# Moving four quantizations into the projection loop of a state-space and FP4 feed-forward layer

## The reference, cut to what matters

```python
def fp4_quant_dequant(x):
    xb = x.reshape(shape[:-1] + (shape[-1] // BLOCK, BLOCK))     # BLOCK = 16
    scale = jnp.max(jnp.abs(xb), axis=-1, keepdims=True) / 6.0
    xn = xb / scale
    idx = jnp.searchsorted(_MID, jnp.abs(xn))
    q = _GRID[idx] * jnp.sign(xn) * scale
...
xn = _layernorm(x, axis=-1)
x = x + _L0_attn_ref(xn, ...) + _L0_ffn_ref(xn, ...)
# _L0_attn_ref: u = layernorm(u, ...); zxbcdt = einsum('bld,od->blo', u, l2norm(in_proj_w)) * DIM ** (-0.5)
# _L0_ffn_ref:  gate = fp4_linear(x, w_gate); y = fp4_linear(x, w_up); fp4_linear(silu(gate) * y, w_down)
```

## Time and profile before

| | us |
|---|---|
| three runs | 13649.85, 13658.45, 13591.88 (median 13649.85) |
| profiled execution, time | 13639.79 |
| its slowest core (core 5), span | 13638.0 |
| the eight cores' spans | 13525.6 to 13638.0 |
| stage 1 on core 5 | about 262 to 2935 |
| busy in the whole span | DVE 6887.7 (51%), PE 6484.3 (48%), PEld 2707.2, ACT 2420.9, POOL 1499.5 |

### The profile page before, as it was taken

The page is one execution under the profiler, slowest core; times in us unless marked ns, Lnnn a source line. Parts: engine busy times, 40 slices in busy tenths (PEclk is TensorE's granted clock), DMA queues, the critical chain, the costliest instruction groups (busy, mean ns, idle before and its releaser), DMA issues.

```text
span 13638.0 us, 120366 instructions; the slowest of 8 cores (13525.6 to 13638.0 us)
## 1 busy us (share of the span) xinstructions
PE 6484.3 (48%) x27434; PEld 2707.2 (20%) x27434; DVE 6887.7 (51%) x21998; ACT 2420.9 (18%) x3604; POOL 1499.5 (11%) x1616
## 2 busy tenths in 40 slices
PE   2555555544555455545554014444444444440678
PEld 1222222212222222222221001111112111110233
DVE  4433333334443444344435986666666666668200
ACT  2222222222222222222222111111111111111000
POOL 1111111100000000000001111111111111111000
PEclk8777777775556555655565556666666666665777
DMA  2111111110001000100010010000000000001232
GB/s 65 45 45 46 46 46 46 45 62 27 30 27 48 27 30 27 48 27 27 30 48 23 31 34 12 12 14 22 12 12 24 12 12 24 12 9 51 98 125 102
DMA packets 285044, 505.71 MB, mean 37 GB/s; under 512 B 35506, under 2 KB 207410, under 8 KB 282306
## 3 DMA queue, kind: packets, MB, share of 16 engines
q1 hardware_dynamic: 235842, 333.82, 7.7%
q0 software_dynamic: 48512, 164.18, 3.1%
HBM read 294.17 MB, written 199.81 MB: 36 GB/s over the span
## 4 chain that ended last, share of the span: by engine, by line
PE 28%; DVE 25%; issue 21%; DMA 14%; ACT 8%; SPq 2%; DVEq 1%; ACTq 0%; POOL 0%; POOLq 0%
DMA s_siluz<-stg_ev 4%; PE p_u L1533 4%; PE p_d L1656 4%; DMA s_xbc<-stg_ev 4%; PE p_g L1524 2%; PE p_sc L1423 2%; PE ptrA L397 2%; DMA hqt<-s_hqT 2%; PE p_seg L1423 2%; DVE hb L1553 2%; DVE q_amax L281 1%; PE ptr L397 1%; ACT q_sg L260 1%; ACT q_absx L259 1%; DVE xbcw L1390 1%
## 5 line engine op out<-in xcount | busy, mean ns | idle before, releaser
L1533 PE MATMUL p_u<-wut,xq 128*128 128x512 bf16 (+1 forms) x3072 | 867.9, 440 | 1422.0 <-DVE hb L1553 1422.0
L716 PE MATMUL pmm<-xhT,wnt 128*128 128x512 bf16 (+1 forms) x4352 | 1149.5, 412 | 736.0 <-ACT stg_ev L733 718.7
L368 POOL TENSOR_TENSOR q_ss<-q_sg,q_sclh 128x512 f16<-128x512 f16 (+3 forms) x560 | 785.5, 1420 | 4899.8 <-DVE q_rcp L291 4714.5
L1524 PE MATMUL p_g<-wgt,xq 128*128 128x512 bf16 (+1 forms) x3072 | 843.9, 428 | 18.4 <-ACT gs L1545 12.1
L1656 PE MATMUL p_d<-wdt,hqt 128*128 128x512 bf16 x2816 | 734.6, 433 | 202.1 <-DVE ostg L1670 201.2
L1545 ACT ACTIVATE gs<-p_g 128x512 bf16<-128x512 f32 (+1 forms) x384 | 213.6, 556 | 3035.9 <-DVE hb L1553 1668.5
L1533 PEld LDWEIGHTS p_u<-wut,xq 128*128 128x128 bf16 x3072 | 343.5, 115 | 1882.3 <-issue 1696.4
L1240 DVE SCALAR_TENSOR_TENSOR attb<-eb,ldtT,scoresM 128x256 bf16<-128x256 bf16 x1024 | 455.0, 485 | 500.3 <-ACT eb L1226 415.2
L1553 DVE TENSOR_TENSOR hb<-p_u,gs 128x512 f32<-128x512 f32 (+1 forms) x384 | 246.6, 642 | 884.7 <-PE p_u L1533 884.7
L1341 POOL TENSOR_TENSOR g2scr<-xbcw 128x256 bf16<-128x256 bf16 x512 | 313.4, 612 | 3418.3 <-DVE xbcw L1327 3418.3
L716 PEld LDWEIGHTS pmm<-xhT,wnt 128*128 128x128 bf16 (+1 forms) x4352 | 408.6, 103 | 1342.2 <-issue 1010.2
(11 more groups left out here) (232 smaller groups left out, 13100.6 us busy)
## 6 DMA issues: line engine op xcount, KB each, us to landing
s_hqT<-hqTb POOLq DMA_DIRECT2D x16, 2816.0 KB, 11.5
hqt<-s_hqT SPq DMA_DIRECT2D x16, 2816.0 KB
xbcw<-s_xbc SPq DMA_DIRECT2D x272, 128.8 KB
s_xbc<-stg_ev SPq DMA_DIRECT2D x272, 128.0 KB
ubuf<-u SPq DMA_DIRECT2D x16, 2048.0 KB
s_siluz<-stg_ev POOLq DMA_DIRECT2D x256, 128.0 KB, 2.0
zld<-s_siluz SPq DMA_DIRECT2D x16, 2048.0 KB
ubp<-u SPq DMA_DIRECT2D x64, 512.0 KB
```

Source lines behind the costliest of these rows:

```text
L368: ii = nc.gpsimd.tensor_mul(q["ss"][:, CS[i]], q["sg"][:, CS[i]], q["sclh16"][:, GS[i]].unsqueeze(2) .broadcast_to([128, hb, 16]))
L716: nc.tensor.matmul(pm[0:rows, :], wnt[:, k * F + ft * 128: k * F + ft * 128 + rows], xhT[:, k * TILE:(k + 1) * TILE], start=(k == 0), stop ...
L1524: i = nc.tensor.matmul(p_g[:, 0:nn], xqb[:, k * TILE + mt * 128: k * TILE + (mt + 1) * 128], wgt[:, k * FFI + i0: k * FFI + i1], start=(k ...
L1533: i = nc.tensor.matmul(p_u[:, 0:nn], xqb[:, k * TILE + mt * 128: k * TILE + (mt + 1) * 128], wut[:, k * FFI + i0: k * FFI + i1], start=(k ...
```

## The change

The four calls of `emit_quant_full` leave their place ahead of the loop over `ft`. They are wrapped in a function `emit_q1` and called at the top of the iterations ft = 1, 9, 17 and 25, ahead of the matmuls of that iteration. In each engine's queue their instructions now stand behind those of ft 0, 8, 16 and 24. `prev_qsg_ac`, for which the next tile's normalization waits, is taken after the last one as before.

```diff
--- before.py
+++ after.py
@@ -687,23 +687,26 @@
                                     pe_waits=[XH_M])
             prev_xht_pe = cnt["pe"]
             qtrans = []
-            for sl4 in range(4):
+
+            def emit_q1(sl4):
                 QS_VE = emit_quant_full(xn[:, sl4 * 1024:(sl4 + 1) * 1024],
                                         qd[:, sl4 * 1024:(sl4 + 1) * 1024],
                                         1024, q1, first_wait=XN_M)
-                if sl4 == 3:
-                    prev_qsg_ac = cnt["ac"]
-                mt = sl4
                 blocks = [(qd[:, sl4 * 1024 + j * 128:
                               sl4 * 1024 + (j + 1) * 128],
-                           xnqT[:, j * TILE + mt * 128:
-                                j * TILE + (mt + 1) * 128])
+                           xnqT[:, j * TILE + sl4 * 128:
+                                j * TILE + (sl4 + 1) * 128])
                           for j in range(8)]
                 qtrans.append((blocks, QS_VE))
+                return cnt["ac"]
 
             xbv = xbc_s.rearrange("(s c p) l -> s c p l", s=SEQ, c=NCT)
             szv = siluz_s.rearrange("(t z p) n -> t z p n", t=NT, z=NZT)
             for ft in range(NFT):
+                if ft % 8 == 1 and ft < 32:
+                    qac = emit_q1(ft // 8)
+                    if ft // 8 == 3:
+                        prev_qsg_ac = qac
                 rows = 128 if ft < 33 else 16
                 pm = (pmm0, pmm1, pmm2)[ft % 3]
                 @block.tensor
```

## The result

The changed kernel takes 13142.4 us, median of 10 runs (13101.7 to 13202.7), against 13623.1 for ten of the kernel before (13566.3 to 13671.3): a ratio of 0.9648, 95% interval 0.9625 to 0.967, 481 us or 3.5% less. The forecast was 13150 us, in the range 13070 to 13290.

A forecast was written before the change was run, and what follows sets the result against it. Waits, not a busy engine, set normalization and input projection, with stores one at a time pacing the ft loop. 34.2-3.0-0.4 = 30.8 us per tile, times 16, took 493 from 13639.8: 13147, stated as 13150, range 13070 to 13290.

The forecast's parts named there:

- The 34.2 us ahead of the second store: Start of each tile's store loop: POOL stores ft 1 at 1472.7 instead of 1506.89, 34.2 us earlier.
- The 3.0 us at ft 9: POOL's queue: quantization 1's `ss` products stand ahead of ft 9's store, 3.0 us lost per tile.
- Stores beside DVE's quantization: POOL's stores: some 8 per tile run beside DVE's quantization, 0.05 us each, 0.4 us lost per tile.
- The bound that I kept for stores beside `aa`: First half of two quantizations: stores waiting out both `aa` would cost 4 us per tile, kept for the range.
- Quantizations 2 and 3 at nothing: Loop's second half, stores on SP: Abs and Sign just fit between ACT's evictions and were costed at nothing.
- The cover of 6 us: End of the loop: quantization 3 ends after 15.1 us while the loop goes on for 21, leaving 6 us.
- Sum: Stage 1: 34.2-3.0-0.4 = 30.8 us saved per tile, times 16: 493 us, giving 13147 us.
- the first: Rival, store loop: more slow transfers, 102 us, 13250, or PE at a reduced clock, 13200; chance 0.08 together.
- Its half about the clock: Store loop: PE at granted clock 0.81 takes 2.67 us per ft, 54 us in all, 13200; joint chance 0.08.
- Stores blocked by DVE: Rival, POOL's stores: each store beside a quantization waits for its end; only 267 us saved, 13370; chance 0.09.
- Cold PE: Rival, projection loop: stalls leave PE at 1.2 GHz throughout, 10 us more per tile, 160 us slower, 13800; chance 0.04.

The follow-up runs named there:

- the kernel at ft = 0: Changed kernel with its four quantizations one iteration earlier, ahead of ft = 0, 8, 16 and 24: 13013.9 us, ratio 0.9561 to the kernel before.
- the yardstick: The changed kernel itself, unaltered, run again beside other runs: 13096.3 us, ratio 0.9627 to the kernel before.
- The kernel at 17, 21, 25: Changed kernel with its quantizations ahead of ft = 1, 17, 21 and 25: 13049.9 us, ratio 0.9592 to the kernel before.
- the last kernel: Kernel before with quantizations at ft = 0, 8, 16, 24, z stores from POOL, x stores from SP, no landing waits in the queues: 12928.4 us, ratio 0.9487.

## Why the prediction was right

**The 34.2 us ahead of the second store** were 33.9 over all tiles (70.20 to 36.33). In the tile shown `amax` starts 2.7 us after ft 0's eviction and `ss` 2.1 after that, and the pair takes 3.02, the steps of the forecast. Two runs show that the store's start is the cause: bringing it 3.75 us further forward gave 3.7 us of period, putting it 4.4 back gave a period 4.4 longer.

**The 3.0 us at ft 9**: the gap between the stores of ft 8 and 9 grew from 2.70 to 5.54 us on average, 2.8; taken away it gave back 2.7 in that stretch. That the mean comes so close to 3.0 is luck. In 14 tiles the loss is 2.3 us (2.60 to 4.88), since `ss` starts a little later and the pair takes 2.6 us; in the other two it is 6.8 (3.42 to 10.21). The forecast had no term for the pair that runs beside DVE's comparisons and takes up to 7.7 us.

**Stores beside DVE's quantization**, 0.05 us each: the store after ft 1's comes 2.60 us later at the median against 2.56 for undisturbed ones, the mean of ft 9's gap to ft 10 is 2.65. The bound that I kept for stores beside `aa` could hardly come about: POOL's own `ss` run beside `aa`, a thing that the order of POOL's queue would have told. Only 16 of the 2048 stores of z touch an `aa`, and their issues took 0.54 to 0.58 us. The Trainium skill (SBUF — State Buffer, section "SBUF: two separate sides") has a DMA from POOL wait for a DVE operation that holds the shared port; no run here shows more than small delays of stores. The longest is that of the kernel at ft = 0, whose second gap is 2.75 at the median, 0.2 over the undisturbed. The lock of the same section of the Trainium skill shows between DVE and POOL's own products: L305 takes 1.13 us beside `ss`, and an operation of its kind 0.28 without it. The 6.87 us of `ss` beside DVE's comparisons fit it too, though no run tells this cause from another. If it is the cause, DVE did hold back a store by way of these products, that of ft 9 in two tiles of sixteen.

**Quantizations 2 and 3 at nothing**: 42.26 and 42.29 us, though the yardstick's 40.68 shows that this stretch is known to some 1.6 us only. The cover of 6 us was 4.9 on average, 2.8 at the least. The kernel at 17, 21, 25 shows what it costs when it is gone.

**Sum**: 30.8 us per tile forecast, 31.1 measured, 493 against 496 us in stage 1. In the total 481 were measured; the slowest core of a run is another each time, and the last stage varied from 867.7 to 965.2 us between the cores of one execution. The time itself came out 8 us from the forecast (5 from the sum, 13147), and that is in part luck: the forecast started from 13639.8, and ten runs of the kernel before have their median at 13623.1, 17 us lower, which happens to offset the 12 us by which the saving fell short.

**The rivals**: the first, 102 us more through slow landings, didn't come. Of the gaps between stores of z, without the two that the change widens, 10.2% were over 3.3 us before and 10.5% after. Its half about the clock was nearer: on cores 6 and 7 of the changed kernel's profile the granted clock stood at 0.81 for 57% of stage 1, against 13% before, and it cost some 2 us of period (133.8 and 135.5 against 132.1 to 133.1 on cores 2 to 5, which had none of it), since the stores were nearly as slow. Stores blocked by DVE: not seen as the rival had it. Cold PE: the share of the projection's matmuls at the low pace fell from 0.12 to 0.07, and making it fall in the kernel before changed nothing.

## What to carry to other kernels

Work moved into the idle time of one engine must be traced in every queue through which it passes: here DVE was the one with the idle time, but the gain was what ACT's and POOL's queues no longer held ahead of the first stores, and the same work put all at once into the loop cost 0.7%. When a loop's pace equals one DMA's issue plus its landing, look at who waits for that landing: that wait in the issuing queue was worth 12 us per tile beside the 31 of the change, and a semaphore for each buffer does without it. Count the cover of moved work at the fastest pace that the loop shows, not at its mean.

## What the runs showed of the hardware

- The granted clock of PE under load was mostly at its two levels, 0.50 (1.2 GHz) and 1.00 (2.4 GHz), but for long stretches at 0.81, which is neither. In stage 1 the 0.81 fell on cores in pairs: 0 and 1, 2 and 3, 4 and 5, 6 and 7 had nearly the same share of the stage at that clock (0.40 and 0.39, 0.00 and 0.00, 0.38 and 0.37, 0.52 and 0.52 in the last kernel; likewise before, after and with all stores on SP). What decides it isn't settled.
- It costs most where PE sets the pace: the last kernel lost 6 to 11 us per tile on such cores, the changed kernel some 2.
- PE kept its full clock over 2.45 us of idleness after 100 one-column matmuls (eight in 1.89 us), while 2.36 us in the kernel before were followed by eight in 3.28. In the kernel before alone, 57 gaps were 2.2 to 2.7 us long: after 13 of them the eight took 1.89 us, after the other 44 they took 2.45 to 4.16. A gap's length alone doesn't tell whether the clock falls.
- POOL's pair of products takes 3.02 us when it starts together with `aa`, and 6.87 when it starts 4.4 us after `amax`, beside DVE's shorter fp16 operations. In the kernel at ft = 0, 8, 16, 24 the pair of quantization 2 starts 4.2 us after `amax` and takes 6.88 at the median. There no store of z waits behind it, and DVE's quantization takes 12.7 us, like the others (12.6).
